# Gated cross-attention block: attention masks added by 32-row tiles of the array, from a mask held four times

## The reference

```python
x = x + tanh(g_xattn) * attention(layernorm(x), ctx, ctx, mask)   # 16 heads of 8
x = x + tanh(g_ffn)   * mixture(layernorm(x))                     # 8 experts, 128 -> 512 -> 128
# inside attention:
scores = einsum('bhqd,bhkd->bhqk', q, k) / sqrt(8)
scores = where(mask[:, None, :, :], finfo.min, scores)
attn   = softmax(scores, axis=-1)
# inside mixture: every expert runs on every token,
# weighted by a thresholded softmax gate
```

## Time and profile before

| | us |
|---|---|
| median of 3 runs | 622.63 |
| lowest and highest run | 621.52, 625.18 |
| the profiled execution | 622.45 |
| its span | 620.6 |
| TensorE (PE) busy | 588.7 |
| VectorE (DVE) busy | 484.4 |
| ScalarE (ACT) busy | 378.5 |

### The profile page before, as it was taken

The page is one execution under the profiler, slowest core; times in us unless marked ns, Lnnn a source line. Parts: engine busy times, 40 slices in busy tenths (PEclk is TensorE's granted clock), DMA queues, the critical chain, the costliest instruction groups (busy, mean ns, idle before and its releaser), DMA issues.

```text
span 620.6 us, 13748 instructions
## 1 busy us (share of the span) xinstructions
PE 588.7 (95%) x4482; PEld 448.7 (72%) x4482; DVE 484.4 (78%) x941; ACT 378.5 (61%) x625; POOL 176.3 (28%) x223
## 2 busy tenths in 40 slices
PE   6689899999999998999999999999999999999998
PEld 5455566666666655788878788787887887887886
DVE  6367677777777776588788889888888888888886
ACT  2144455555555554867776767676777676776773
POOL 5443444444453221112203212212112112122121
PEclk9799899999999999999999999999999999999999
DMA  5865554556555420051111221121121121121210
GB/s 142 244 172 157 162 161 141 142 155 170 161 152 158 142 55 5 6 103 51 43 60 35 64 60 52 51 66 40 46 68 51 37 64 51 51 64 38 68 51 17
DMA packets 43998, 55.12 MB, mean 89 GB/s; under 512 B 9520, under 2 KB 27824, under 8 KB 42416
## 3 DMA queue, kind: packets, MB, share of 16 engines
q1 hardware_dynamic: 43504, 53.99, 31.0%
q10 hardware_dynamic: 448, 0.53, 0.3%
HBM read 39.16 MB, written 14.81 MB: 87 GB/s over the span
## 4 chain that ended last, share of the span: by engine, by line
PE 78%; DMA 4%; ACT 4%; DVE 2%; SPq 2%; issue 2%; ACTq 0%; DVEq 0%
PE ps_h L1033 10%; PE ps_h L1035 9%; PE ps_h L1034 9%; PE ps_y L1048 9%; PE ps_y L1050 9%; PE ps_y L1049 9%; DMA kq_st<-maxT 4%; PE misc L1011 4%; PE scores L949 3%; PE scores L977 3%; PE scores L989 2%; PE scores L966 2%; ACT probs L541 1%; PE misc L1088 1%; PE misc L1180 1%
## 5 line engine op out<-in xcount | busy, mean ns | idle before, releaser
L565 ACT ACTIVATE h_sb<-ps_h,b_sb 128x512 f32<-128x512 f32 x256 | 175.9, 689 | 102.3 <-PE ps_h L1035 92.2
L709 DVE TENSOR_TENSOR h_low<-h_sb,h_high 128x512 fp32r<-128x512 f32 x256 | 164.6, 683 | 0.1
L504 POOL TENSOR_TENSOR yT<-yT,weighted 128x512 f32<-128x512 f32 x54 | 70.9, 1313 | 277.8 <-DVE weighted L891 277.8
L705 DVE CAST h_high<-h_sb 128x512 fp32r<-128x512 f32 x128 | 97.9, 765 | 52.6 <-ACT h_sb L565 52.4
L686 DVE TENSOR_REDUCE neg_max<-scores 128x8 f32<-128x1024 f32 x64 | 77.9, 1222 | 42.3 <-PE scores L949 42.3
L1033 PE MATMUL ps_h<-x_high,w_high 128*128 (+1 forms) x256 | 101.8, 398 | 2.1 <-ACT h_sb L565 2.0
L1048 PE MATMUL ps_y<-h_high,w_high 128*128 128x512 f32 x256 | 100.2, 391 | 0.3 <-ACT h_high L569 0.3
L1035 PE MATMUL ps_h<-x_high,w_low 128*128 (+1 forms) x256 | 99.8, 390 | 0.0
L1034 PE MATMUL ps_h<-x_low,w_high 128*128 (+1 forms) x256 | 99.7, 390 | 0.0
L1050 PE MATMUL ps_y<-h_high,w_low 128*128 128x512 f32 x256 | 99.7, 389 | 0.0
L1049 PE MATMUL ps_y<-h_low,w_high 128*128 128x512 f32 x256 | 99.6, 389 | 0.0
(11 more groups left out here) (127 smaller groups left out, 716.0 us busy)
## 6 DMA issues: line engine op xcount, KB each, us to landing
w_row<-w_scratch SPq DMA_DIRECT2D x64, 256.0 KB, 3.1
kq_st<-kq_scratch SPq DMA_DIRECT2D x64, 192.0 KB
kq_scratch<-kq_parts SPq DMA_DIRECT2D x30, 256.0 KB, 3.5
w_raw<-in_w_ffn SPq DMA_DIRECT2D x16, 256.0 KB, 3.3
kq_scratch<-kq_parts SPq DMA_DIRECT2D x32, 128.0 KB, 3.5
ctx_sb<-in_ctx SPq DMA_DIRECT2D x16, 128.0 KB, 2.7
out_y<-y_out SPq DMA_DIRECT2D x7, 256.0 KB, 2.3
x_all<-in_x SPq DMA_DIRECT2D x13, 128.0 KB, 2.2
```

Of the source, the lines that this page charges most:

```text
L504: nc.gpsimd.tensor_tensor(yT[:], yT[:], weighted[:, e % 2, :], ALU.add).then_inc(added, 1)
L565: nc.scalar.activation(h_sb[:, j % HBUF, :], ps_h[:, j % 4, :], ACT.Gelu_apprx_tanh, bias=b1_sb[:, j:j + 1]).then_inc(h_done, 1)
L705: nc.vector.tensor_copy(h_high[:, j % HBUF, :], h_sb[:, j % HBUF, :]).then_inc(high_odd, 1)
L709: nc.vector.tensor_tensor(h_low[:, j % HBUF, :], h_sb[:, j % HBUF, :], h_high[:, j % HBUF, :].bitcast(F32), ALU.subtract).then_inc(low2_do ...
```

## The change

Four things change together.

1. **The mask matmuls.** One matmul over 128 rows and 128 columns of the array becomes, for each row block r, four over 32 rows. Natural: a tile of 32 rows by 32 columns for each of four query blocks `j`, 512 columns streamed, eight for a pair of banks where there were two. Transposed: a tile of 32 rows by 128 columns, with 128 columns streamed (four slabs of 32 queries), again eight for a pair where there were two.
2. **The mask's layout.** Row block r needs all 128 queries in its own 32 rows. So `mask_words` and `mask_b` hold, in each of the four row blocks, a full copy: row i of a block has the queries 4i to 4i + 3 (`j` = 0 to 3) side by side. The mask of a group is loaded by four DMAs of 32 rows (512 bytes in one piece) where there was one of 128 rows (128 bytes in one piece), and the CAST handles 1024 elements on a partition where there were 256.
3. **The queries' order.** Query 4i + j goes to position 32j + i: the transposes of `xn` write their columns in that order (`dealt`), and the two ACT copies into `headsT` put them back.
4. **Space.** `mask_words`, `merged`, `mergedT` and `x2n` have one buffer where they had two, so the waits before their writers name group g - 1 where they named g - 2, and the mask of group g + 1 is loaded in round g, once POOL's CAST of group g is done.

```diff
-        mask_words = sa("mask_words", [P, 2, GB, S // 4], I32)
-        mask_b = sa("mask_b", [P, 2, GB, S], BF16)
+        mask_words = sa("mask_words", [P, GB, S], I32)
+        mask_b = sa("mask_b", [P, 2, GB, 4, S], BF16)
...
-            mask_v = a["mask"].rearrange("(g b) q k -> g q b k", b=GB)
+            mask_v = a["mask"].rearrange("(g b) (i j) k -> g i b (j k)", b=GB, j=4)
...
+            def load_mask(g):
+
+                for r in range(ROWS):
+                    sp.dma_start(mask_words[32 * r:32 * r + 32, :, :], mask_v[g]).then_inc(mask_in[g % 2], 16)
+
...
-                    if g > 0:
-                        wait_count(sp, mask_done, g - 1)
-                        sp.dma_start(mask_words[:, u, :, :], mask_v[g]).then_inc(mask_in[u], 16)
-                if (g := group_at(it, 1)) is not None:
-                    u = g % 2
+                if (g := group_at(it, 1)) is not None:
+                    u = g % 2
+                    if g > 0:
+                        sp.wait_ge(mask_done, g)
+                        load_mask(g)
...
-                    if g >= 2:
-                        misc_wait_full(act, "wo", g - 2)
-                    nc.scalar.activation(mergedT[:, u, :], misc[:, bank_of("merged"), 0:GT], ACT.Copy).then_inc(misc_read[bank_of("merged")], 1)
+                    if g >= 1:
+                        misc_wait_full(act, "wo", g - 1)
+                    nc.scalar.activation(mergedT[:], misc[:, bank_of("merged"), 0:GT], ACT.Copy).then_inc(misc_read[bank_of("merged")], 1)
...
-                    nc.scalar.activation(headsT[:, 0, :], misc[:, bank_of("V0"), 0:2 * P], ACT.Copy).then_inc(misc_read[bank_of("V0")], 1)
+                    nc.scalar.activation(headsT[:, 0, :].rearrange("p (k i j) -> p k j i", k=2, j=4),
+                                         misc[:, bank_of("V0"), 0:2 * P].rearrange("p (k j i) -> p k j i", k=2, j=4), ACT.Copy).then_inc(misc_read[bank_of("V0")], 1)
...
-            def natural_mask(r, b, u):
-                return mm(scores[:, r, :].rearrange("p (s k) -> p s k", s=SLABS), masked_ident[:],
-                          mask_b[:, u, b, :].unsqueeze(1).to_broadcast([P, SLABS, S]), start=False, stop=True)
+            def natural_mask(pair, b, u):
+
+                for j in range(4):
+                    for r in pair:
+                        rows = slice(32 * r, 32 * r + 32)
+                        ins = mm(scores[32 * j:32 * j + 32, r, :].rearrange("p (s k) -> p s k", s=SLABS), masked_ident[rows, rows],
+                                 mask_b[rows, u, b, j, :].unsqueeze(1).to_broadcast([32, SLABS, S]), start=False, stop=True)
+                return ins
...
-            def transposed_mask(r, b, u):
-                return mm(scores[:, 2 + r, :].rearrange("p (s q) -> p s q", s=SLABS), mask_b[:, u, b, :],
-                          masked_ident[:].unsqueeze(1).to_broadcast([P, SLABS, S]), start=False, stop=True)
+            def transposed_mask(pair, b, u):
+
+                for j in range(4):
+                    for r in pair:
+                        rows = slice(32 * r, 32 * r + 32)
+                        ins = mm(scores[:, 2 + r, :].rearrange("p (s j i) -> p j s i", s=SLABS, j=4)[:, j], mask_b[rows, u, b, j, :],
+                                 masked_ident[rows, rows].unsqueeze(1).to_broadcast([32, SLABS, 32]), start=False, stop=(j == 3))
+                return ins
```

More of the change, by code:

```diff
@@ L148, in gated_block @@
         sums_r = sa("sums_r", [P, GB * H], F32)
-        merged = sa("merged", [P, 2, GB * H, HD], F32)
-        mergedT = sa("mergedT", [P, 2, GT], F32)
+        merged = sa("merged", [P, GB * H, HD], F32)
+        mergedT = sa("mergedT", [P, GT], F32)
         x_biased = sa("x_biased", [P, GB, D], F32)
@@ L154, in gated_block @@
         rstd2 = sa("rstd2", [P, 2, GB], F32)
-        x2n = sa("x2n", [P, 2, GB, D], F32)
+        x2n = sa("x2n", [P, GB, D], F32)
         x2T = sa("x2T_sb", [P, 2, GT], F32)
@@ L308, in wait_spare_loads @@
                 eng.wait_ge(ctx_in[u], 8 * NG)
-                eng.wait_ge(mask_in[u], 8 * NG)
+                eng.wait_ge(mask_in[u], 32 * NG)
                 eng.wait_ge(w_in[u], 8 * NG)
@@ L635, in body @@
                         misc_wait_full(act, "heads", g - 1)
-                    nc.scalar.activation(headsT[:, 1, :], misc[:, bank_of("V1"), 0:2 * P], ACT.Copy).then_inc(misc_read[bank_of("V1")], 1)
+                    nc.scalar.activation(headsT[:, 1, :].rearrange("p (k i j) -> p k j i", k=2, j=4),
+                                         misc[:, bank_of("V1"), 0:2 * P].rearrange("p (k j i) -> p k j i", k=2, j=4), ACT.Copy).then_inc(misc_read[bank_of("V1")], 1)
                     if g == NG - 1:
@@ L760, in body @@
                     dve.wait_ge(recip_done, g + 1)
-                    if g >= 2:
-                        misc_wait_full(dve, "merged", g - 2)
-                    nc.vector.tensor_tensor(merged[:, u, :, :], hv[:, :, 0:HD], sums_r[:].unsqueeze(2).to_broadcast([P, GB * H, HD]),
+                    if g >= 1:
+                        misc_wait_full(dve, "merged", g - 1)
+                    nc.vector.tensor_tensor(merged[:], hv[:, :, 0:HD], sums_r[:].unsqueeze(2).to_broadcast([P, GB * H, HD]),
                                             ALU.mult).then_inc(misc_read[bank_of("heads")], 1)
@@ L830, in body @@
                     dve.wait_ge(rstd2_done, g + 1)
-                    if g >= 2:
-                        misc_wait_full(dve, "x2T", g - 2)
+                    if g >= 1:
+                        misc_wait_full(dve, "x2T", g - 1)
                     for b in range(GB):
-                        nc.vector.tensor_scalar(x2n[:, u, b, :], x_all[:, g * GB + b, :],
+                        nc.vector.tensor_scalar(x2n[:, b, :], x_all[:, g * GB + b, :],
                                                 mean_var2[:, u, b, 0:1], rstd2[:, u, b:b + 1], ALU.subtract, ALU.mult).then_inc(x2n_done, 1)
@@ L934, in _, with dealt @@
             mm = nc.tensor.matmul
+            def dealt(t):
+                return t.rearrange("p (j i) -> p i j", j=4)
             def turn(what, g, src, n=GB):
@@ L939, in turn @@
                 for b in range(n):
-                    ins = nc.tensor.transpose(misc[:, k, b * S:(b + 1) * S], src(b), ident[:])
+                    out = misc[:, k, b * S:(b + 1) * S]
+                    ins = nc.tensor.transpose(dealt(out) if b >= GB else out, src(b), ident[:])
                 ins.then_inc(misc_full[k], 1)
@@ L990, in transposed @@
                            start=(s == 0), stop=False)
[L991 to L992 removed]
+                transposed_mask((0, 1), b, u).then_inc(tr_low_full, 1)
             def transposed_rest(g, b, u):
[L996 to L997 removed]
+                transposed_mask((2, 3), b, u).then_inc(tr_rest_full, 1)
             def values(g, b, u):
@@ L1072, in body @@
                         pe.wait_ge(g_copied, 1)
-                    turn("x2T", g, lambda b: x2n[:, u, b, :])
+                    turn("x2T", g, lambda b: x2n[:, b, :])
                     if g == NG - 1:
@@ L1087, in body @@
                     for b in range(GB):
-                        ins = mm(misc[:, bank_of("wo"), b * D:(b + 1) * D], mergedT[:, u, b * S:(b + 1) * S], wo_sb[:], start=True, stop=True)
+                        ins = mm(misc[:, bank_of("wo"), b * D:(b + 1) * D], mergedT[:, b * S:(b + 1) * S], wo_sb[:], start=True, stop=True)
                     ins.then_inc(misc_full[bank_of("wo")], 1)
```

14 lines of the change are left out of this document (6 added, 8 removed).

## The result

The changed kernel takes 658.95 us (median of 4 runs, 656.48 to 669.51) where the kernel before takes 623.48 (4 runs): 1.0542 times as long, 95% interval 1.0474 to 1.0609. It is slower, as forecast, but by 35 us, not by 7; 659 lies 22 us above the range.

What follows compares the result with a forecast made beforehand. Attention was taken to be bound by two loops of about equal length, SP with DMA and PE. Round and start terms summed to +5.6, clock dips added +1.5: 622.45 + 7.1 = 629.6 us, range 618.5 to 636.5.

Steps and rivals of the forecast that it cites:

- What bounds the kernel: In attention, an SP and DMA loop of 13.84 us closes on a PE loop of about the same length.
- The extra mask DMAs: Ahead of the kq_st loads, three more issues cost 1.35 us, moving the batch-0 maxima's landing by about +1.15 us.
- rounds that I had counted as covered: In four other rounds up to round 11, PE's lateness eats most of the delay: +0.15 each, 0.6 us.
- The masks' matmuls on the path: Between the maxima's landing and SP's next issue, sixteen transposed masks take 0.6 us for 0.97, a gain of 0.37 per round.
- The masks' matmuls off the path: Natural masks and batch-1 transposed ones: savings don't shorten a round, they lengthen PE's wait; a pair may take 0.5 to 1.9 us.
- three such dips at 0.5: +1.5: TensorE's clock falls behind PE's waits, grown to 1.5 to 2 us; three dips add 1.5 us.
- The rest: CAST grows from 0.41 to 1.2 to 1.6 us, costing nothing; copies up to 0.1 us each off the path; start +0.3.
- The drain between tiling modes: Changing tiling mode drains the array; six more changes a round would give back 0.6 us of PE's time.
- The signs: In the changed profile: slower mask issues and loads, SP's wait nearly gone, PE waiting in about ten rounds, early rounds 14.4 to 14.8 us.
- Rival 3: Small tiles cost as well: each transposed step takes 0.17 us, 8 us more, 637 us; chance 0.14.
- Rival 2: PE sets the pace, so all mask savings count: 0.9 us a round, 609 or some 616 us; chance 0.12.

Runs made afterwards that it cites:

- Run 15: Kernel before with the loads of x, ctx, w_raw and the mask issued behind the batch-0 maxima from round 1 on; 619.61 us, ratio 0.9929.
- run 13: Kernel before with each group's mask load split into four DMAs of 32 rows in the same place; 644.26 us, ratio 1.0307.
- run 8: Changed kernel with masks in the old shape and its four mask DMAs issued behind the batch-0 maxima; 626.85 us, ratio 1.0058.
- e1: Changed kernel with all mask matmuls in the old whole-array shape, four mask DMAs kept ahead of the kq_st loads; 642.96 us, ratio 1.0328.
- e3: Changed kernel with masks in the old shape and one mask DMA instead of four; 624.57 us, ratio 1.0037.
- e2: Changed kernel with one mask DMA of the same 128 KB instead of four, small tiles kept; 655.18 us, ratio 1.0495.
- e11: Changed kernel with small tiles for the transposed masks alone, natural ones in the old shape, four mask DMAs behind the batch-0 maxima; median 647.88 us.
- 12: Changed kernel with small tiles for the natural masks alone, transposed ones in the old shape, four mask DMAs behind the batch-0 maxima; 627.95 us, ratio 1.0040.
- 6: Changed kernel with small tiles for the transposed masks alone, natural ones in the old shape, two mask DMAs; 653.40 us, ratio 1.0477.
- 7: Changed kernel with small tiles for the natural masks alone, transposed ones in the old shape, two mask DMAs; 664.63 us, ratio 1.0653.
- e9: Complete changed kernel with its four mask DMAs issued behind the batch-0 maxima; 664.85 us, ratio 1.0588.
- e10: Changed kernel with mask DMAs behind the batch-0 maxima, plus two whole-array zero matmuls ahead of each pair's tiles, 256 in all; 660.62 us, ratio 1.0538.
- e14: Kernel before without its 256 mask matmuls, DMAs, CAST and layouts unchanged; 639.91 us, ratio 1.0233.
- e4: Changed kernel plus one whole-array zero-weight matmul ahead of each natural pair's eight tiles, 64 in all; 672.37 us, ratio 1.0789.
- e5c: Changed kernel with one mask DMA and no mask matmuls; median 649.13 us, ratio 1.0239.

## Why the prediction was wrong

**What bounds the kernel**: right, as far as it went. Two loops close on each other, and SP's queue ahead of the `kq_st` loads is one of them. Run 15 shortened that queue and gained 4 us, the size of PE's waits; run 13 lengthened it in the kernel before, and run 8 took the longer one away again. What it left out is that PE's loop has no fixed length: it holds only at the clock that was granted.

**The extra mask DMAs**: the mechanism was right, the size too small. The term was 1.35 us of issue and +1.15 us of landing in a round; in most rounds the issues took 1.84 us for four, 1.4 more than one, but up to 2.9 more in some (runs 1 and 13). Summed up without the masks' gain it would have been 7 x 1.15 + 0.6 = 9 us; alone it measured 18 (e1 against e3), 16 (e1 against e8) and 21 (e13). What is missing is those long issues, the clock behind the longer waits (0.96 to 0.98 in e1 and e13), and rounds that I had counted as covered (ten and eleven waits for seven). How the gap divides among the three wasn't measured.

**The masks' matmuls on the path**: 0.6 us for sixteen was high, they take 0.41 at full clock, and 0.15 to 0.37 us of idle time for DVE's `v_pad` may follow. The gain in PE's time was there. It didn't matter.

**The masks' matmuls off the path**: here the prediction failed. "These savings don't shorten a round" was right; the step from that to a cost of nothing was wrong. The work taken away was whole-array work, a quarter of PE's time in attention with the masks on the path counted in, and with it went the clock. That is worth 31 us from e3 to e2 with one mask DMA, and 16 us from e1 to the changed kernel with four, so its share of the 35 us depends on which change is counted first; either way the forecast had 0 for it. In the sum, the clock had one term, "three such dips at 0.5: +1.5", and it hung on PE's waits alone. In the changed kernel, PE ran at 1.2 GHz through stretches without any wait.

**The rest**: the CAST took 1.04 us, under my 1.2 to 1.6, off the path. The copies into `headsT`, which I gave up to 0.1 us, grew from 0.38 to 0.62 and 0.64 us, and PE waits 6.5 us for the second of them in 14 rounds, where it had no such wait before; with everything else they cost 2 us or less (e3).

**The drain between tiling modes**, weighed by the Trainium skill's page "TensorEngine Tiling (Array Packing)", Key Properties, didn't show as a loss: a natural pair with both its hand-overs takes 0.33 to 0.42 us at full clock (0.33 from 178.42, 0.42 from 185.51) where two whole-array masks with theirs took 0.44 to 0.54.

**The signs**: the four issues (0.43 us each) and the first load 4.69 us behind the batch-1 maxima came as forecast. SP's wait before the batch-0 maxima, which was to be nearly gone, is 23.7 us; PE waits for them in six rounds instead of ten; and the round shown takes 15.98 us, not 14.4 to 14.8. These three point at a slower PE.

**The rivals**: none named what happened. Rival 3 came nearest in time (637) and mentioned a clock that falls in every round only in passing. Rival 2 counted on tiles that run side by side. They do, as the 0.33 us for eight of 512 columns show, and that is what took the work away.

What stays open: what of the whole-array work counts for the clock (rows, columns, type and place weren't separated), why the transposed tiles cost the clock so much more than the natural ones (11 against 12), why two DMAs that fetch four copies each brought the maxima later than four DMAs did (6, 7), and why e9 is 10 us slower than e2.

## What to carry to other kernels

Before making matmuls smaller, look at what stands around them: in a stage of small matmuls, a few whole-array ones may be what keeps TensorE at 2.4 GHz, and 55 us of them could be put back for nothing here (e10) and were missed dearly where they had gone (e14). But a quarter of that work, in one place, gave nothing back and cost its full time (e4). So price an edit of PE's work at both clocks, and look at the clock of the stretch first when a result surprises. And in a round whose loads hang on one queue, count the issues ahead of the load that is waited for: three more DMAs there cost 16 to 21 us, behind it 2, and moving the spare ones back gained 0.7%.

## What the runs showed that I had not expected

- The kernel before without its 256 mask matmuls is about 16 us slower (ratio 1.0233), at clock 0.70 in attention instead of 0.99 in the profiles (0.87 and 0.986 over the whole kernels).
- Whole-array matmuls with zero weights or zero moving values keep the clock up as the real ones did: 0.98 to 0.99 over the whole kernel with 256 of them (e10), 0.86 to 0.89 without (e9). With 64 of them it stayed at 0.90 (e4).
- Time and clock go closely together between executions of one kernel: in e5c 635.2 us at 0.906, 641.4 at 0.891, 656.9 at 0.851, 663.5 at 0.837; in e11 634.6 at 0.962 and 655.7 at 0.924.
- PE can be busy without a gap for 6.7 us and stay at 1.2 GHz (the changed kernel, 216.00 to 222.70), and can idle 0.96 of 3 us and stay at 2.4 GHz (e3, 221.20 to 224.20).
- Eight matmuls on tiles of 32 by 32 with 512 columns take 0.33 to 0.42 us together with the hand-over, at full clock; two whole-array ones take 0.44 to 0.54.
- An ACT copy of 128x256 whose output steps by four elements took 0.62 to 0.64 us where the plain one took 0.38.
